# Layer 1's attention written out with two convolution passes, and two-byte tables in the routing

## The chip, the cores and the metric

The kernel runs on one core of a Trainium2 chip. The metric is device time in microseconds (us) of one execution. TensorE (PE, matrix products), VectorE (DVE), ScalarE (ACT), GpSimd (POOL) and SyncE (SP, which here only issues DMAs) run side by side and wait for each other through semaphores. Each engine works through its own instructions in order.

## The reference, cut to what matters

A batch of 16 samples with 102 tokens of 192 features goes through four layers, each an attention and a feed-forward part. The change touches the attention of layer 1 and the routing ahead of the experts in layers 0 and 1.

```python
# layer 1, attention (12 heads of 16 features); then h = h + out
qkv = layernorm(h, ln_g, ln_b) @ qkv_w.T + qkv_b             # q, k, v
attn = einsum('bhnd,bhmd->bhnm', q, k) * D ** (-0.5)
kernel = ones((3, 3)); kernel[1, 1] = 0                      # the eight neighbours
neigh = conv(attn, kernel, padding='SAME')
attn = softmax(attn - 0.2 * neigh)
out = einsum('bhnm,bhmd->bhnd', attn, v)

# layers 0 and 1, feed-forward: 8 experts, the best 2 of each token
top_logits, top_idx = top_k(xn @ gate_w, 2)
y = sum over the two of  gate * (act(xn @ w1[e]) @ w2[e])    # 1632 tokens x 2 = 3264 rows
```

The convolution needs no pass over the scores. The 3x3 sum of q.k is (sum of three neighbouring q).(sum of three neighbouring k), so each head takes 32 partitions instead of 16: the first 16 hold q and 1.2 k, the other 16 hold the sums of three q and -0.2 times the sums of three k.

## The kernel before, in words

`build` runs the layers one after the other, each in a block that all engines enter and leave together.

**Layer 1's attention**, `neighbour_attention` (L1020), works on pairs of samples, 8 pairs, "n" or "i" being the pair and "j" or "side" the sample in it. For each pair POOL gathers the experts' results of layer 0 back (`take_rows_back`, 4 indirect DMAs, L1294). DVE adds them into `h` (`add_rows_back`, L1329), takes mean and variance (`begin`), POOL raises the variance to -0.5 (`norm.pool`, L269), and DVE scales the rows into `z` (`end`, L264). PE transposes `z` (L1102), ACT copies the result to `xT` (L1220). PE multiplies it with the weights for q, k (`projected`, L1109, three blocks of 128 outputs for each) and v (`values`, L1122), and always splits the 192 inputs into two halves of 96. ACT copies q and k to `raw_q` and `raw_k` (L1226). DVE makes `qT` and `kT` from them in three passes (`mix`): raw times an own weight (L1353), plus the left neighbour (L1355), plus the right one (L1358).

For each sample PE then forms the scores (`scores`, L1137), DVE takes the maxima (L1364), PE turns them (L1145), ACT copies them (L1244), PE forms the scores again by key (L1153) and subtracts the maxima (L1158), ACT takes the exponentials (L1249), PE multiplies with v (`outputs`, L1167), ACT copies (L1254), PE turns back (`outputs_back`, L1176), DVE divides by the sums (L1371, L1373) and adds to `h` (`add_up`, L1379).

The order is written out by hand as a software pipeline. A prologue enters pairs 0 to 2, and then PE, ACT and DVE each run a loop of four rounds (`Fori(0, B // 4)`, L1198, L1265, L1402) over two pairs. Step i, j of the loop handles the output of sample 2i+j, the scores of the next sample, the projections of pair i+2 and the entry of pair i+3. The loop runs the same for all pairs, so in the last rounds it also handles pairs 8, 9 and 10, which hold zeros (`PADS`). PSUM is shared: the scores of the next sample overwrite the banks in which the q blocks (or k blocks) of pair i+2 stood, so `scores` waits for ACT's copies of them, and for DVE's copy of v (L1345).

**The routing**, in `routed_experts` (L2176), turns the two chosen experts of each token into a list of 33 tiles of 128 rows. DVE works out a slot for each token and choice. Then it writes two tables as 0 and 1 in bf16: `at_tile` (which of 33 tiles, L2587, multiplied with sample and token numbers into `named`, L2590 and L2592) and `at_row` (which of 128 rows, four instructions, L2595). PE multiplies them, 32 products (L2425), which gives the token of each slot; DVE makes `tokens` from it (L2610, L2612), POOL gathers the rows of the first tiles (L2344), and PE starts with the experts (L2356, L2368). After the tables DVE also works out which expert owns each tile (`owner`, L2599 to L2607); SP waits for it (`owner_ready`) to load the first three tiles' weights (L2288). PE waits for `tokens_ready` and then runs 12 dummy products (`fill`, L131), which write what nobody reads. Before that PE has 28 more at the start of the block, as `neighbour_attention` has 60.

Of the kernel before, what the change touches and what calls it, by code (L numbers as in the profile page):

```python
# [74 lines left out]
    "l1a": [("wq", K, C * HT * 128), ("wk", K, C * HT * 128), ("wv", K, C * D), ("bq", 128, HT), ("bk", 128, HT),  # L75
            ("bv", L, D), ("g", K, C), ("b", K, C), ("mix", 128, 4)],
# [29 lines left out]


class Steps:

    def __init__(self, eng, sem, before=0):
        self.eng, self.sem, self.before, self.n = eng, sem, before, 0

    def done(self, ins):
        ins.then_inc(self.sem, 1)
        self.n += 1

    def wait(self):
        self.eng.wait_ge(self.sem, self.before + self.n)  # L120
# [111 lines left out]


class Norm:


    def __init__(self, m, g, name, twice=False):
        times = 1 + twice
        self.twice = twice
        self.stats = m.sb(name + "_stats", [L, 2, 6])  # L240
        self.moments = m.sb(name + "_moments", [L, 2, 2])
        self.shifted = m.sb(name + "_shifted", [L, times, 2])
        self.rstd = m.sb(name + "_rstd", [L, times, 2])
        self.pause = m.sb(name + "_pause", [1, 1])
        self.neg_half = g["const"].at("neg_half16")[:, 0:2 * times].rearrange("p (a n) -> p a n", a=times)
        self.var_ready, self.rstd_ready = m.sem(name + "_var_ready"), m.sem(name + "_rstd_ready")

    def begin(self, dve, steps, src):

        for j in range(2):  # L250
            steps.done(dve.bn_stats(self.stats[:, j, :], src[j]))
        steps.wait()
        dve.memset(self.pause[:, :], 0.0)
        for j in range(2):
            steps.done(dve.bn_aggr(self.moments[:, j, :], self.stats[:, j, :]))
        steps.wait()
        last = dve.tensor_scalar(self.shifted[:, 0, :], self.moments[:, :, 1], EPS, None, ALU.add)
        if self.twice:
            last = dve.tensor_scalar(self.shifted[:, 1, :], self.moments[:, :, 1], 1.0 + EPS, EPS * EPS, ALU.mult, ALU.add)
        last.then_inc(self.var_ready, 1)  # L260
# [759 lines left out]
def neighbour_attention(nc, g, phase, experts):  # L1020
# [12 lines left out]
    with ExitStack() as stack:  # L1033
# [35 lines left out]
        def banked(j):  # L1069

            return ps[0:L, j, :, 0:HT * L].rearrange("p r (t n) -> p r t n", t=HT)
# [2509 lines left out]
```

## Time and profile before

| | us |
|---|---|
| median of 3 runs | 1826.01 |
| lowest and highest | 1823.01, 1833.23 |
| the profiled execution's own time | 1823.17 |
| its span | 1821.5 |
| layer 0's routing, within the span | 193.6 to 239.7 |
| layer 1's attention, within the span | 395.8 to 559.4 |
| layer 1's routing, within the span | 559.4 to 608.0 |

The profile is one execution recorded by the hardware. Its page has a table of busy time by engine and a strip of the span in 40 slices. The trace can be asked for groups of instructions by line, for who waited for whom, for the instructions in order of time, and for the busy time within given stretches, with the TensorE clock that was granted there (1.00 is 2.4 GHz, 0.50 is 1.2 GHz).

### The profile page before, as it was taken

To read this page: it belongs to the slowest core of one execution; us is meant where nothing else is said; L and a number is where in the kernel's file an instruction comes from. 1 tells how busy PE (TensorE), PEld (TensorE's weight loads), DVE (VectorE), ACT (ScalarE), POOL (GpSimd) and SP (SyncE) were. 2 spreads that over 40 slices of the span, in tenths; PEclk is the share of its full clock that TensorE was granted. 3 is DMA by queue.
4 is the path that set the end of the run, shared out by engine and by line. 5 is a ranking of instruction groups with operands and counts; after the bars stand their busy time and mean duration, and the time that the engine had idled before them with its cause. 6 is when DMAs were issued, how large, how long until landed. Compare 5 with 4: busy or idle time off the path is not lost. (4 is left out here: it accounts for less than half of the span.)

```text
span 1821.5 us, 35955 instructions
## 1 busy us (share of the span) xinstructions
PE 1619.2 (89%) x13405; PEld 1136.1 (62%) x13425; DVE 1020.2 (56%) x2819; ACT 749.2 (41%) x1439; POOL 557.3 (31%) x530
## 2 busy tenths in 40 slices
PE   7999689997996799979888877999999998889996
PEld 5677479976775699757645553222224775558886
DVE  2487722225888322258525665888886776942221
ACT  1266123323542111135524544899994553211111
POOL 1231022226001242265101112555553101325543
PEclk9999689997997899979889999999999998989998
DMA  6000445521004455212010114999992004026662
GB/s 227 1 2 2 159 159 182 183 88 44 1 0 163 158 182 182 91 29 76 35 46 1 42 51 138 385 395 370 360 327 103 2 2 151 4 72 187 187 186 35
DMA packets 97448, 228.04 MB, mean 125 GB/s; under 512 B 24298, under 2 KB 55754, under 8 KB 96394
## 3 DMA queue, kind: packets, MB, share of 16 engines
q1 hardware_dynamic: 77527, 206.13, 32.0%
q0 software_dynamic: 19552, 19.63, 4.4%
q8 instruction: 100, 1.64, 0.4%
q14 instruction: 59, 0.48, 0.1%
q10 hardware_dynamic: 210, 0.15, 0.0%
HBM read 198.91 MB, written 26.56 MB: 124 GB/s over the span
## 5 line engine op out<-in xcount | busy, mean ns | idle before, releaser
L2845 ACT ACTIVATE l2s_hidden<-ps,pack_l2f 128x816 f32<-128x816 f32 x256 | 226.8, 937 | 19.0 <-PE ps L2769 9.7
L2864 POOL TENSOR_TENSOR l2s_gated<-l2s_hidden,l2s_whole 128x408 f32<-128x408 f32 x128 | 136.7, 1068 | 104.0 <-PE ps L2777 104.0
L2887 DVE TENSOR_TENSOR l2s_gated<-l2s_hidden,l2s_whole 128x816 f32<-128x816 f32 x128 | 143.4, 1120 | 28.1 <-ACT l2s_hidden L2845 25.1
L2344 POOL DMA_INDIRECT l_xt<-rows_in,l_tokens x66 | 63.2, 957 | 250.8 <-PE ps L2357 193.6
L2385 PE MATMUL ps<-l_down,l_hidden 128*128 x792 | 139.8, 327 | 0.0
L2385 PEld LDWEIGHTS ps<-l_down,l_hidden 128*128 128x128 f32 x792 | 127.3, 190 | 0.4
L131 PE MATMUL ps<-pack_const 128*128 128x512 bf16 x366 | 98.2, 427 | 22.7 <-PEq L165 6.0
L2368 PE MATMUL ps<-l_xtT,l_up 128*128 128x128 f32 x792 | 101.2, 278 | 3.4 <-DVE l_xtT L2620 3.4
L2368 PEld LDWEIGHTS ps<-l_xtT,l_up 128*128 128x128 f32 x792 | 98.2, 194 | 4.5 <-DVE l_xtT L2620 4.5
L2464 ACT ACTIVATE l_hidden<-ps,l_down 128x128 f32<-128x128 f32 x198 | 54.6, 375 | 91.6 <-PE ps L2373 91.6
L3199 POOL DMA_INDIRECT out<-l3c_part,l3c_chosen_place x32 | 57.1, 1785 | 98.6 <-DVE l3c_part L3318 90.0
L3156 ACT ACTIVATE l3c_expert_gate<-ps 128x204 f32<-128x204 f32 x96 | 27.5, 338 | 145.1 <-PE ps L3092 145.1
L131 PEld LDWEIGHTS ps<-pack_const 128*128 128x128 bf16 x386 | 40.0, 107 | 75.5 <-issue 41.2
L2467 ACT ACTIVATE l_hidden<-ps 128x384 f32<-128x384 f32 x66 | 28.8, 488 | 139.7 <-PE ps L2373 139.7
L3328 DVE TENSOR_TENSOR l3c_expert_hidden<-l3c_expert_gate,ps 128x204 f32<-128x204 f32 x96 | 30.9, 364 | 98.1 <-ACT l3c_expert_gate L3156 98.1
L2880 DVE TENSOR_TENSOR l2s_gated<-l2s_hidden,ps 128x408 f32<-128x408 f32 x128 | 73.3, 572 | 15.5 <-ACT l2s_hidden L2845 9.9
L2620 DVE TENSOR_SCALAR l_xtT<-ps,pack_l0r 128x128 f32<-128x128 f32 x66 | 24.1, 406 | 78.6 <-PE ps L2357 78.6
L2620 DVE TENSOR_SCALAR l_xtT<-ps,pack_l1r 128x128 f32<-128x128 f32 x66 | 24.0, 406 | 77.8 <-PE ps L2357 77.8
L3105 PE MATMUL ps<-l3c_wd,l3c_expert_hidden 128*102 128x192 f32 x384 | 65.0, 326 | 0.0
L2791 PE MATMUL ps<-l2s_gated,early_down 128*32 128x408 f32 x512 | 58.5, 530 | 5.0 <-POOL l2s_gated L2864 3.5
L2373 PE MATMUL ps<-l_xtT,l_up 64*128 64x128 f32 x792 | 62.7, 291 | 0.0
L3105 PEld LDWEIGHTS ps<-l3c_wd,l3c_expert_hidden 128*102 128x102 f32 x384 | 61.4, 168 | 0.2 <-issue 0.2
(514 smaller groups left out, 3664.0 us busy)
## 6 DMA issues: line engine op xcount, KB each, us to landing
l2s_whole<-g_whole SPq DMA_DIRECT2D x128, 612.0 KB, 7.1
l_up<-in_l_up SPq DMA_DIRECT2D x66, 576.0 KB, 3.8
l3c_wg<-in_l_gate SPq DMA_DIRECT2D x16, 576.0 KB, 4.9
l3c_wu<-in_l_up SPq DMA_DIRECT2D x16, 576.0 KB, 6.5
l3c_wd<-in_l_down SPq DMA_DIRECT2D x16, 576.0 KB, 3.9
slots_out<-l_y SPq DMA_DIRECT2D x66, 96.0 KB, 2.3
l_down<-in_l_down SPq DMA_DIRECT2D x8, 675.0 KB, 7.9
l_down<-in_l_down SPq DMA_DIRECT2D x8, 576.0 KB, 8.0
```

Of the source, the lines that this page charges most:

```text
L131: pe.matmul(bank, halves[:, 0:128], halves[:, :], start=True, stop=True)
L2344: pool.indirect_dma_start(xt[:, i % 3, :], None, xs, bass.IndirectOffsetOnAxis(ap=tokens[:, i:i + 1], axis=0))\
L2368: pe.matmul(hid_bank(i, half)[:, t * 128:(t + 1) * 128], up[:, i % 3, n * 128:(n + 1) * 128], xtT[:, i % 2, 0, :], start=(t == 0), stop=Fa ...
L2373: last = pe.matmul(hid_bank(i, half)[:, t * 128:(t + 1) * 128], up[rows, i % 3, F + t * 128:F + (t + 1) * 128], xtT[rows, i % 2, 1, :], st ...
L2385: last = pe.matmul(y_bank(i), hidden[:, i % 2, t, :], wd[:, t * D:(t + 1) * D], start=(t == 0), stop=(t == FM - 1))
L2791: last = pe.matmul(sums[row:row + HP, :], down[2 * r + odd][:, pair, t, :], gated[:, (4 * n + 2 * pair + c) % ring, :], start=(odd == 0 an ...
L2845: act.activation(hidden[:, p % kept, :, :], ps[:, 0, 2 * (p % 2):2 * (p % 2) + 2, 0:NG], ACT.Gelu_apprx_tanh, bias=w.at("b1")[:, s * MT + ...
L2864: pool.tensor_tensor(gated[:, (4 * n + 1) % ring, :], hidden[:, 2 * n % kept, 1, :], whole[:, n % ahead, 0, :], ALU.mult).then_inc(late_re ...
L2880: dve.tensor_tensor(gated[:, 4 * n % ring, :], hidden[:, 2 * n % kept, 0, :], gate_bank(n), ALU.mult).then_inc(gated_ready, 1)
L2887: dve.tensor_tensor(gated[:, at:at + 2, :], hidden[:, (2 * n + 1) % kept, :, :], whole[:, n % ahead, 1:3, :], ALU.mult).then_inc(gated_rea ...
L3105: last = pe.matmul(part_bank(e)[:, a * D:(a + 1) * D], expert_hidden[:, e % 2, t, a, :], wd[:, e % RING, t, :], start=(t == 0), stop=(t == ...
L3199: pool.indirect_dma_start(table, bass.IndirectOffsetOnAxis(ap=chosen_place[:, a, e:e + 1], axis=0), part[:, e % 2, a, :], None, compute_op ...
```

## The change

**Layer 1's attention.** The loops become plain code for 16 samples (`for s in range(B)`), and the work on pairs 8 to 10 is gone. The 192 inputs are split into 128 and 64: a product over 128 rows, and one over 64 rows that is placed in the upper or lower half of the array, so that two of them (one with v, one with q or k; or two blocks) can stand beside each other. The 64-feature half of z is turned by products with the identity into both halves of the partitions. The k weight (1.2 and -0.2) goes into ACT's copy, `raw` gets a zero column at both ends, and the own-weight pass is gone: two passes remain. ACT takes the exponentials of sample 0 before it copies q and k of pair 1. POOL takes over `h += o` (`add_up`), DVE's division waits for it two samples later (`h_added`), and POOL issues the gathers of pair i+4 at step i instead of all at the start. The norm keeps three sets of moments (`PairNorm`, which the other attentions use already).

**The routing.** The tables are laid out with 8 tokens innermost, and all their operands become two bytes wide: `rows_8` and `sample_8` are made by POOL at the start of the block, `splitf` is bf16. PE reads the tables with a step of 8 elements. The owners are worked out before the ranks, and the fill has 10 products and stands before the wait for `tokens_ready`.

```diff
 # neighbour_attention, tensor engine
-                for c in range(C):
-                    for j in range(2):
-                        last = pe.transpose(zT_at(side)[:, ...], z[:, par, j, c * K:(c + 1) * K], ident[0:L, 0:L])
+                for j in range(2):
+                    pe.transpose(zT_at(side)[:, j * L:(j + 1) * L], z[:, n % 2, j, 0:WIDE], ident[0:L, 0:L])
+                for j in range(2):
+                    for a in range(2):
+                        last = pe.matmul(zT_at(side)[half_rows(a), (2 + j) * L:(3 + j) * L], z[:, n % 2, j, WIDE:D],
+                                         ident[0:L, 0:L], start=True, stop=True, tile_position=(0, REST * a))
+            def first_block(wt, side, j, bank=2):
+                pe.matmul(v_at(side, bank), xT[:, 0, j, :], wv[:, 0, :], start=True, stop=False)
+                wide_part(wt, side, 0)
+                pe.matmul(v_at(side, bank), xT[half_rows(0), 1, j, :], wv[half_rows(0), 1, :], start=False, stop=True,
+                          tile_position=(0, 0)).then_inc(v_ps, 1)
+                rest_part(wt, side, 0, 1)
+            def other_blocks(wt, side, done):
+                for t in (2, 1):
+                    wide_part(wt, side, t)
+                rest_part(wt, side, 2, 1)
+                rest_part(wt, side, 1, 0).then_inc(done, 1)
 # its order at the start
+            first_block(wq, 1, 0, bank=2)
+            scores_by_key(0)
+            other_blocks(wq, 1, q_ps)
             pe.wait_ge(q_ready, 2)
+            first_block(wk, 1, 1, bank=3)
+            other_blocks(wk, 1, k_ps)
-            with pe.Fori(0, B // 4) as two:
+            for s in range(B):
+                n, j = s // 2 + 2, s % 2
+                outputs(s)
+                if n < pairs and not j:
+                    transposes(n, 0)
+                if s + 1 < B:
+                    scores(s + 1)
+                outputs_back(s)
+                if n < pairs:
+                    pe.wait_ge(xT_ready, n + 1)
+                    first_block(wk if j else wq, j, j)
+                if s + 1 < B:
+                    top_turned(s + 1)
+                    scores_by_key(s + 1)
+                if n < pairs:
+                    other_blocks(wk if j else wq, j, k_ps if j else q_ps)
 # scalar engine: exponentials_by_key(0) now ahead of q_copies(1, 1) and k_copies(1)
 # GpSimd
+            def add_up(s):
+                pool.wait_ge(o_ready, s + 1)
+                pool.tensor_tensor(h[:, s, :], h[:, s, :], o[:, s % 2, :], ALU.add).then_inc(h_added, 1)
+            for i in range(pairs):
+                if i + 4 < pairs:
+                    take_rows_back(i + 4)
+                for j in range(2):
+                    add_up(2 * i + j)
+                if i + 3 < pairs:
+                    norm.power(pool, i + 3)
 # vector engine, mix
-                steps.done(dve.tensor_scalar(dst, raw, own_w, None, ALU.mult))
-                dve.scalar_tensor_tensor(dst[:, :, 1:L], raw[:, :, 0:L - 1], side_w, dst[:, :, 1:L], ALU.mult, ALU.add)
-                dve.scalar_tensor_tensor(dst[:, :, 0:L - 1], raw[:, :, 1:L], side_w, dst[:, :, 0:L - 1], ...)
+                dve.scalar_tensor_tensor(dst, raw[:, :, 0:L], beside, raw[:, :, 1:L + 1], ALU.mult, ALU.add)
+                dve.scalar_tensor_tensor(dst, raw[:, :, 2:L + 2], beside, dst, ALU.mult, ALU.add)
 # routed_experts
+            pool.tensor_copy(rows_8[:, :, :], iota.unsqueeze(2).broadcast_to([L, 128, 8])).then_inc(counted, 1)
+            pool.tensor_copy(sample_8[...], const.at("sample")).then_inc(counted, 1)
-                last = pe.matmul(ps[:, 1, 2, 0:2 * TILES], at_row[:, n, :], named[:, n, :, :], ...)
+                last = pe.matmul(ps[:, 1, 2, 0:2 * TILES], at_row[:, n // 8, :, n % 8], named[:, :, n // 8, :, n % 8], ...)
             last.then_inc(tokens_ps, 1)
+            fill(pe, g, ps[:, 0, 0, :], 10)
             pe.wait_ge(tokens_ready, 1)
-            fill(pe, g, ps[:, 0, 0, :], 12)
 # vector engine: the four owner instructions (L2599 to L2607) now ahead of the rank (L2569)
-            for n in range(0, 2 * B, 8):
-                dve.tensor_tensor(at_row[:, n:n + 8, :], iota.unsqueeze(1).broadcast_to([L, 8, 128]),
-                                  splitf[:, 1, n:n + 8].unsqueeze(2).broadcast_to([L, 8, 128]), ALU.is_equal)
+            for n in range(4):
+                dve.tensor_tensor(at_row[:, n, :, :], rows_8[:, :, :],
+                                  splitf[:, 1, n, :].unsqueeze(1).broadcast_to([L, 128, 8]), ALU.is_equal)
```

## Rows read from the trace of the kernel before

**Rows 1.** Waits, 447 to 559 us: waiter <- releaser: total us, times, longest.

```profile
PE ps L1137 <- ACT l1a_raw_q L1226: 3.4, 4, 0.9
```

**Rows 2.** Groups by line, VectorE, 447 to 559.2: count, busy, mean ns.

```profile
L1379 DVE TENSOR_TENSOR h<-h,l1a_o 102x192 f32 x16 | 5.6, 349 | 0.0
...
L1353 DVE TENSOR_SCALAR l1a_qT<-l1a_raw_q,pack_l1a 128x612 f32<-128x612 f32 x8 | 4.3, 533 | 0.0
```

**Rows 3.** Order of time, two samples of the loop: start, duration, engine, line.

```profile
464.53 0.80 PE L1137 MATMUL ps<-l1a_kT,l1a_qT 32*102 32x102 f32 x24 [0.79 <-DVE l1a_v L1345]
...
470.89 0.56 PE L1102 MATMUL ps<-pack_const,l1a_z 102*96 102x102 f32 x4
...
471.85 0.80 PE L1137 MATMUL ps<-l1a_kT,l1a_qT 32*102 32x102 f32 x24 [0.40 <-ACT l1a_raw_k L1226]
...
476.10 1.25 ACT L1249 ACTIVATE l1a_pT<-ps 102x612 f32<-102x612 f32 x2 [0.90 <-PE ps L1158]
...
477.72 1.07 ACT L1226 ACTIVATE l1a_raw_q<-ps,pack_l1a 128x204 f32<-128x204 f32 x3 [0.38 <-PE ps L1109]
...
479.12 0.80 PE L1137 MATMUL ps<-l1a_kT,l1a_qT 32*102 32x102 f32 x24 [0.85 <-ACT l1a_raw_q L1226]
```

**Rows 4.** Order of time, first output, first and second scores of the loop.

```profile
438.11 0.74 PE L1167 MATMUL ps<-l1a_pT,l1a_v 102*32 102x102 f32 x24 [2.48 <-ACT l1a_pT L1249]
...
440.64 1.38 PE L1137 MATMUL ps<-l1a_kT,l1a_qT 32*102 32x102 f32 x24
...
450.23 0.80 PE L1137 MATMUL ps<-l1a_kT,l1a_qT 32*102 32x102 f32 x24 [0.85 <-ACT l1a_raw_q L1226]
```

**Rows 5.** By stretch: us, busy of five engines, granted clock, DMA share, GB/s.

```profile
440.00:447.00 7.00, 7.00 (x74) 5.85 (x73) 4.80 (x9) 1.35 (x3) 5.48 (x6) 0.60 0.18 46
...
454.20:468.50 14.30, 13.45 (x212) 10.76 (x208) 12.35 (x34) 6.93 (x16) 1.04 (x1) 1.00 0.01 2
...
241.00:242.00 1.00, 1.00 (x7) 0.78 (x8) 0.00 (x0) 0.00 (x0) 0.00 (x0) 0.50 0.24 78
```

**Rows 6.** Order of time, last output, last division, next block's start.

```profile
549.60 0.73 PE L1167 MATMUL ps<-l1a_pT,l1a_v 102*32 102x102 f32 x24
...
559.48 0.11 DVE L2517 MEMSET l_before<- 102x64 f32 x1 [0.36 <-PEq L1033]
```

**Rows 7.** Order of time, layer 0's attention: split products, POOL's addition.

```profile
115.56 0.57 PE L597 MATMUL ps<-pack_const,l0f_z 102*64 102x102 f32 x8
...
120.63 1.59 PE L607 MATMUL ps<-l0f_xT,pack_l0f 128*128 128x204 f32 x8
...
109.49 0.96 PE L612 MATMUL ps<-l0f_xT,pack_l0f 64*128 64x204 f32 x8
...
110.79 0.86 POOL L861 TENSOR_TENSOR x<-x,pack_l0f 102x384 f32<-102x384 f32 x1
```

**Rows 8.** Order of time, layer 0's routing.

```profile
224.11 1.26 DVE L2590 TENSOR_TENSOR l_named<-x,pack_const 102x1056 bf16<-102x1056 bf16 x1
...
225.28 0.49 DVE L2592 TENSOR_SCALAR l_named<-x,pack_const 102x1056 bf16<-102x1056 bf16 x1
...
225.69 4.62 DVE L2595 TENSOR_TENSOR x<-pack_const,l_splitf 102x1024 bf16<-102x1024 f32 x4
...
231.67 0.20 DVE L2612 SCALAR_TENSOR_TENSOR l_tokens<-l_token_sums 128x33 uint32<-128x33 f32 x1
...
238.43 0.30 PE L2356 MATMUL ps<-pack_const,l_xt 128*128 128x128 f32 x1 [1.21 <-DMA l_xt<-rows_in,l_tokens]
```

**Rows 9.** Order of time, layer 1's routing: owners, tokens, first transposes.

```profile
600.21 0.41 DVE L2599 TENSOR_TENSOR l_passed<-pack_const,l_tiles_of 1x264 f32<-1x264 f32 x1
...
601.64 0.20 DVE L2612 SCALAR_TENSOR_TENSOR l_tokens<-l_token_sums 128x33 uint32<-128x33 f32 x1
...
606.72 0.30 PE L2356 MATMUL ps<-pack_const,l_xt 128*128 128x128 f32 x1
```

More of the change, by code:

```diff
@@ L231, in _ @@
                 dve.tensor_tensor(emb[:, q, :], ps[0:GB * NP, 0, q, 0:D], bias[:, :], ALU.add).then_inc(emb_ready, 1)
[L234 to L248, printed above, removed]
-        for j in range(2):
[L251 to L260, printed above, removed]
-    def apply(self, dve, i, src, dst, time=0):
-        dve.wait_ge(self.rstd_ready, i + 1)
-        return [dve.tensor_scalar(dst[j], src[j], self.moments[:, j, 0:1], self.rstd[:, time, j:j + 1],
-                                  ALU.subtract, ALU.mult) for j in range(2)]
-    def pool(self, pool, i):
-        pool.wait_ge(self.var_ready, i + 1)
-        pool.tensor_tensor(self.rstd[:, :, :], self.shifted[:, :, :], self.neg_half, ALU.pow).then_inc(self.rstd_ready, 1)
 def retention(nc, g, dram):
@@ L1284, in relay @@
                 sp.sem_inc(rows_back, 1)
-            for n in range(B // 2):
+            for n in range(pairs):
                 relay(n)
-            sp.sem_inc(rows_back, PADS // 2)
         @block.gpsimd
@@ L1317, in _ @@
-            dve.sem_inc(o_ready, freed)
-            enter_own = 10
-            def pair(n):
-                return [ds(2 * n + j, 1) for j in range(2)]
-            def add_rows_back(n, steps):
+            steps = Batch(dve, dve_steps)
+            dve.tensor_scalar(k_bias[:, :], w.at("bk"), w.at("mix")[:, 1:2], None, ALU.mult).then_inc(const_ready, 1)
+            for raw in (raw_q, raw_k):
+                last = dve.memset(raw[:, :, :, :], 0.0)
+            last.then_inc(const_ready, 1)
@@ L1347, in mix @@
[L1347 to L1351 removed]
+                dve.tensor_tensor(v[:, n % 2, j, :, 0:HD], heads, w.at("bv", H), ALU.add).then_inc(v_ready, 1)
@@ new lines, in entered @@
+            def entered(n):
+                add_rows_back(n)
+                begin(n)
+                end(n)
+            entered(0)
+            entered(1)
+            kept_values(0, 0, 0, 3)
+            kept_values(0, 1, 1)
+            mix(0, 0)
+            mix(0, 1)
+            maxima(0)
+            entered(2)
+            kept_values(1, 0, 1, 2)
+            mix(1, 0)
+            kept_values(1, 1, 1, 3)
+            for s in range(B):
+                i, j = s // 2, s % 2
+                if s + 1 < B:
+                    maxima(s + 1)
+                divide(s)
+                if j:
+                    if i + 3 < pairs:
+                        begin(i + 3)
+                    if i + 2 < pairs:
+                        kept_values(i + 2, 1, 1)
+                    if i + 3 < pairs:
+                        end(i + 3)
+                    if i + 2 < pairs:
+                        mix(i + 2, 0)
+                else:
+                    if i + 1 < pairs:
+                        mix(i + 1, 1)
+                    if i + 3 < pairs:
+                        add_rows_back(i + 3)
+                    if i + 2 < pairs:
+                        kept_values(i + 2, 0, 0)
```

457 lines of the change are left out of this document (194 added, 263 removed).

## Prediction, made before the changed kernel was run

> **What bounds the kernel now.** I read the trace in this order. First the order of time, to find the stages that the change touches: layer 1's attention, and in layers 0 and 1 the stretch from the choice of experts to the first tile. Together they are 258 of 1821.5 us, and the rest of the program stays as it is. Then the waits and the groups by line in the attention, the loop sample by sample, and its two ends.
>
> In the loop, VectorE and TensorE are both nearly full: 12.35 and 13.45 of 14.30 us, at clock 1.00 [rows 5]. But neither share is the bound. The reader is to look at what ends the wait of the scores (L1137), because each sample's scores start the next round of a ring: scores, maxima, turning, subtraction, exponentials, outputs, next scores. From 464.53 to 471.85 is 7.32 us and from 471.85 to 479.12 is 7.27 us [rows 3]. At 464.53 the scores waited for VectorE's copy of v, at 479.12 for ScalarE's copies of q, whose exponentials had ended at 477.35; the latter happens in every second pair [rows 1, 3]. So VectorE and ScalarE are late in turns, and an edit that relieves one of them leaves the other. From the second scores at 450.23 to the last outputs at 549.60 are 99.4 us [rows 4, 6], that is 13 samples at 7.21 and 5.7 us from scores to outputs.
>
> At the start, the first outputs (438.11) waited 2.48 us for exponentials, the scores of sample 1 then ran at the low clock (1.38 us against 0.80), and 9.6 us passed to the next ones [rows 4, 5]. At the end, 9.9 us pass between the last outputs and the next block, though the last division is over at 554.0 [rows 6]: the rest is work on pairs that don't exist.
>
> **The change, part by part.** All sums are against the profiled execution: 1823.17 us, with 1821.5 us of span.
>
> *The loop.* VectorE loses two own-weight passes of 0.53 us and two additions of 0.35 us for each pair, 1.8 us in all [rows 2]. That ends the waits for its copy of v. The additions go to GpSimd, where half of the 0.86 us that 384 columns took is 0.43 us [rows 7], beside four gathers for each pair; the division waits for them two samples later, some 14 us, so I cost this wait at nothing. If GpSimd came late by more than that, each microsecond would count fully. What is late next is ScalarE's copies of q. They waited 0.38 us for TensorE's last blocks [rows 3]. These blocks took 1.65 us; now they are two wide products, 1.59 / 4 = 0.40 us each, and two of 64 rows, 0.96 / 4 = 0.24 us each [rows 7], together 1.3 us, over before the exponentials end. So that step falls from 7.27 to 6.9 us. The other step contains the transposes: 0.56 us now [rows 3], and then half of that for the 128 wide part and 0.57 us for the rest [rows 7], 0.3 us more, starting at 470.89: scores at 471.75 instead of 471.85, 7.2 us. A pair costs 14.1 instead of 14.4 to 14.6; I take 13.95, since the loop's own turn also goes. The bounds are 14.5 (another wait takes over) and 13.3 (scores right behind outputs, with neither copies nor transposes late). Five pairs to sample 12 save 2.3 us. Samples 13 to 15 have no projections, copies or transposes ahead of their scores, and take about 6.35 us instead of 7.21: 2.6 us. Sum: **-4.9 us**, bounds -2 and -8.
>
> *Its start.* The two removed passes lie on the way to the first scores (-1.0 us). The exponentials of sample 0 now run beside the projections of pair 1, and the 2.48 us wait goes [rows 4]; against that stand the turning with more products and a longer wait for the copies of q. I get the scores of sample 1 about 3.3 us earlier. If the clock is then up, the 9.6 us to the next scores become 7.3: -2.3 us more [rows 4, 5]. Taken: **-5 us**, bounds -2 (clock still down) and -7.
>
> *Its end.* After the last outputs (0.73 us) come a copy, turning back, the division, and GpSimd's addition. Today the division ends 4.4 us after the outputs start, with the maxima of a seventeenth sample and copies of q in the way. I put it at 2.6 us, plus 0.5 for the addition and 0.35 for the change of block: 3.4 instead of 9.9 us [rows 6]. **-6.5 us**, bounds -4.6 (division as late as now) and -7.
>
> *The routing, twice.* The tables are two instructions of 1056 columns and four of 1024. The slope of such an instruction between 192 and 1056 columns is (1.26 - 0.35) / (1056 - 192) = 1.05 ns a column [rows 2, 8]. Half of that is 0.55 us for each of six: -3.3 us. No row shows a two-tensor instruction at two columns a beat. The bounds are nothing gained, and the one-tensor form's 0.49 us for 1056 columns [rows 8], -4.5 us; I take the half, since two tensors have to be read.
>
> The Trainium skill, VectorE: DVE Perf Modes, perf-mode tier table, has `tensor_tensor` at twice the rate when all operands are two bytes wide and at the single rate otherwise. The row that this can be held against has bf16 result and table but an f32 factor, and took 1.26 us [rows 8], which agrees with its second half. By the rule the six cost what I take.
>
> TensorE now reads both tables with a step of 16 bytes. Its products are eight for each `at_row` instruction and fit in its 1.16 us today; at 0.6 us they would be the bound if slowed. No row has such a read. I take no loss, and up to +2.4 us a layer as the bound (a doubled time for the products).
>
> The Trainium skill, SBUF: State Buffer, section on its two separate sides, says that SBUF has lines of 16 bytes, and that each access which crosses to a new line pays. Here each element would. By it the saving in the tables could vanish; this is the third rival.
>
> The owners, 1.2 us from 600.21 to the end of their four instructions [rows 9], move ahead of the tables. There they delay everything, while now they overlap PE's last products in part: +0.85 us. In return SP can load the first three tiles' weights some 9 us earlier, on idle DMA queues. POOL's `rows_8` copy comes before the first variance and is hidden. Behind the tokens, the first transposes came 6.8 us later in layer 0, waiting for the gather, and 5.1 us in layer 1, behind 12 dummy products [rows 8, 9]. With weights out of the way and the fill ahead of the wait, I take 4.6 us for both: -2.2 and -0.5 us. Sum for the two layers: -6.6 + 1.7 - 2.7 = **-7.6 us**, bounds +3 and -11.
>
> Together -4.9 - 5 - 6.5 - 7.6 = -24 us: 1799.2 us against the profiled 1823.17. The median before is 2.8 us above that execution, the lowest run 0.2 below. I put the changed kernel's median at **1801 us**, 1.4% below the median before.
>
> **The rivals.**
> 1. *The ring is shorter than I think*: with VectorE relieved, the scores follow right behind the outputs, 13.3 us a pair, and the clock stays up at the start. For it: VectorE stood in several rings at once. Against: ScalarE's copies of q come after the exponentials in any case [rows 3]. Another -5: 1796 us.
> 2. *The start stays cold and the loop keeps its 14.4 us*, because a copy or the longer transposes replace the wait for v. Then only the ends, the last samples and the routing gain: -2.6 - 2 - 6.5 - 7.6, 1804 to 1806 us.
> 3. *The tables gain nothing*: single rate, or TensorE's stepped reads as the new bound. The routing then gives about -1 instead of -7.6: 1808 us. With the clock falling in layer 1 too, 1810. In layer 0 it fell to 0.50 at 241 us, in the midst of the first tile, after TensorE had stood before and behind the first transposes [rows 5, 8]; now the fill ends earlier in both. I price it at what the cold start cost one sample, 2.3 us [rows 4].
> 4. *Slower*: the written-out attention runs at the low clock. TensorE is less dense than 13.45 of 14.30 us, since two 64-row products share the array. Cold, a sample took 9.6 instead of 7.3 us [rows 4, 5]; for 13 samples +30 us: 1831 us. It decides once about a third of the samples run cold, 24 / 2.3 = 10 of them for no gain at all. Against it: the fall at 440 us came after a wait of 2.48 us and another for the transposes, and the ring leaves TensorE no gap over about 1 us.
> 5. *The change doesn't do what it says*, as when the written-out code stalls on its instructions. Layer 0's attention is written out and shows no such waits. About 1823.
>
> **How the numbers follow.** Forecast 0.57 (1796 to 1806), rival 1 0.12, rival 2 0.12, rival 3 0.12, rival 4 0.04, rival 5 0.03. The range is 1790 to 1812: it takes in rivals 1 to 3 and most of the bounds. A change of 0.5%, 9 us, is about what a measurement of this kernel can tell from none. Forecast and rivals 1 to 3 all lie below 1817, so faster 0.92, same 0.04, slower 0.04.
>
> **What would show each step.** In the changed profile: L1167 to the next block's start about 3.4 us; scores to scores 6.9 and 7.2 us in the loop and 6.35 for the last three; the own-weight pass gone and the second scores near 445; clock 1.00 from there; the `at_row` comparisons at 0.6 us and the eight products behind them still at 0.6; the first transposes 4.6 us behind the tokens. I would be wrong if the wait of the scores moved to a place that I did not name, if the tables kept their 1.15 us, or if the clock in the attention fell below 1.00 after 450 us.

## The result, and the profile after

Eleven runs of the changed kernel have a median of 1813.1 us, ten of the kernel before 1827.4 us (an eleventh took 5250 us and is left out of the ratio). The ratio is 0.9936, 95% interval 0.9913 to 0.9960. A second series of twelve runs gave 1816.5 against 1826.7 us, 0.9930 (0.9904 to 0.9957). So the change makes the kernel faster by 0.65 to 0.7%, about 12 us. I had forecast 24 us and 1801 us, with a range up to 1812: the sign was right, the size half of what I had said, and the median lies just above the range.

The profiled execution of the changed kernel took 1823.34 us (span 1821.3), as long as the profiled one of before. To see why, I cut both spans where TensorE's first instruction of each block starts. "Touched" are the three blocks that the change touches, "others" is the rest of the span, whose code is the same.

| us | routing and experts, layer 0 | attention, layer 1 | routing and experts, layer 1 | touched | others |
|---|---|---|---|---|---|
| before | 202.1 | 163.6 | 201.6 | 567.3 | 1254.2 |
| after | 198.0 | 160.9 | 200.2 | 559.1 | 1262.2 |

The touched blocks gained 8.2 us and not 24. In this pair of executions the 8.2 us are taken up again by 8.0 us more in identical code. The largest piece of it stands in one place, the last 14 us ahead of the block at 1398 us. The windows (columns: stretch, its length, busy time and count of PE, PEld, DVE, ACT, POOL, PE's granted clock, DMA share, GB/s) of the kernel before and of the changed one:

```profile
1384.00:1398.00 14.00, 12.01 (x55) 7.13 (x58) 5.60 (x10) 2.27 (x4) 0.29 (x1) 1.00 0.00 0
```

```profile
1377.00:1398.00 21.00, 19.41 (x66) 10.58 (x59) 6.38 (x12) 2.27 (x4) 0.82 (x3) 0.67 0.00 0
```

The changed kernel reached these products 6.6 us earlier, then ran most of them at the low clock, and left them 0.8 us earlier.

**The attention's end.** TensorE's instructions in the order of time, from the scores of sample 13 on (start, duration, engine, line, operation, and in brackets how long the engine had stood and for whom). L1093 are the scores, L1127 the outputs:

```profile
522.69 0.80 PE L1093 MATMUL ps<-l1a_kT,l1a_qT 32*102 32x102 f32 x24 [1.08 <-ACT l1a_raw_k L1201]
525.10 0.48 PE L1101 MATMUL ps<-pack_const,l1a_top 102*128 102x102 f32 x3 [1.15 <-DVE l1a_top L1334]
528.25 1.25 PE L1127 MATMUL ps<-l1a_pT,l1a_v 102*32 102x102 f32 x24 [1.37 <-ACT l1a_pT L1212]
529.42 1.38 PE L1093 MATMUL ps<-l1a_kT,l1a_qT 32*102 32x102 f32 x24
538.08 1.37 PE L1093 MATMUL ps<-l1a_kT,l1a_qT 32*102 32x102 f32 x24
545.54 1.25 PE L1127 MATMUL ps<-l1a_pT,l1a_v 102*32 102x102 f32 x24 [1.37 <-ACT l1a_pT L1212]
```

The reader is to see three gaps of 1.08, 1.15 and 1.37 us within 7 us, where transposes and projections used to stand, and the next products at 1.25 us instead of 0.73: the clock is down. The window of the tail, before and after, has 1.00 and 0.51 (the last number but two):

```profile
527.00:552.00 25.00, 22.87 (x369) 18.32 (x368) 21.27 (x51) 12.93 (x31) 1.32 (x2) 1.00 0.00 0
```

```profile
527.00:552.00 25.00, 15.06 (x199) 10.13 (x199) 5.02 (x11) 5.82 (x11) 1.76 (x3) 0.51 0.00 1
```

The last scores come 8.66 us behind the ones before, not 6.35. The same step takes 8.64 to 8.66 us in each of the eight other profiles of this code without dummy products in the tail. Behind the last outputs follow GpSimd's addition and the next block:

```profile
548.96 0.59 POOL L1262 TENSOR_TENSOR h<-h,l1a_o 102x192 f32<-102x192 f32 x1 [6.75 <-DVE l1a_o L1345]
552.49 1.04 POOL L2286 CAST l_rows<-pack_const 102x1024 bf16<-102x1024 f32 x1 [2.94 <-POOLq L978]
552.52 8.95 PE L116 MATMUL ps<-pack_const 128*128 128x512 bf16 x28 [4.30 <-PEq L978]
```

The addition ends at 549.55, and nobody starts for 2.9 us. Before, VectorE's last instruction ended at 559.11 and the next block began at 559.48 [rows 6]:

```profile
558.26 0.85 DVE L1358 SCALAR_TENSOR_TENSOR l1a_qT<-l1a_raw_q,pack_l1a,l1a_qT 128x606 f32<-128x606 f32 x1
```

**Its start.** The clock fell while the first projections ran; four products took 1.73 us where they take 0.96 at 519 us. Below them the window of five microseconds behind:

```profile
407.17 0.57 PE L1065 MATMUL ps<-pack_l1a,l1a_xT 128*102 128x192 f32 x2 [1.39 <-ACT l1a_xT L1182]
409.04 1.73 PE L1055 MATMUL ps<-l1a_xT,pack_l1a 128*128 128x204 f32 x4
...
420.37 1.38 PE L1093 MATMUL ps<-l1a_kT,l1a_qT 32*102 32x102 f32 x24 [2.02 <-DVE l1a_kT L1329]
```

```profile
410.00:415.00 5.00, 5.00 (x17) 3.07 (x16) 2.21 (x11) 1.07 (x3) 3.48 (x4) 0.50 0.13 32
```

**Its loop.** The rows of one pair. From 479.49 to 486.59 are 7.10 us, to 494.05 7.46 us; the usual pair of steps is 7.10 and 7.37:

```profile
479.49 0.80 PE L1093 MATMUL ps<-l1a_kT,l1a_qT 32*102 32x102 f32 x24 [0.26 <-issue]
483.94 1.34 DVE L1300 SCALAR_TENSOR_TENSOR h<-rows_z,share,h 102x192 f32<-102x192 f32 x2
484.13 0.60 POOL L1262 TENSOR_TENSOR h<-h,l1a_o 102x192 f32<-102x192 f32 x1
485.99 0.35 DVE L1318 TENSOR_TENSOR l1a_v<-ps,pack_l1a 102x192 f32<-102x192 f32 x1
486.59 0.80 PE L1093 MATMUL ps<-l1a_kT,l1a_qT 32*102 32x102 f32 x24 [0.81 <-DVE l1a_v L1318]
494.05 0.80 PE L1093 MATMUL ps<-l1a_kT,l1a_qT 32*102 32x102 f32 x24 [0.35 <-DVE l1a_qT L1329]
```

**The tables**, in layer 1's routing (L2565 `at_tile`, L2573 the four `at_row`, L2393 TensorE's 32 products, L2580 the tokens, L2324 the first transposes):

```profile
587.09 0.71 DVE L2565 TENSOR_TENSOR x<-l_rows,l_splitf 102x1056 bf16<-102x1056 bf16 x1
588.86 2.50 DVE L2573 TENSOR_TENSOR x<-l_rows,l_splitf 102x1024 bf16<-102x1024 bf16 x4
589.69 4.17 PE L2393 MATMUL ps<-l_named,x 102*128 102x66 bf16 x32 [9.11 <-DVE x L2573]
593.90 0.23 DVE L2578 COPY l_token_sums<-ps 128x66 f32<-128x66 f32 x1 [2.54 <-PE ps L2393]
594.16 0.20 DVE L2580 SCALAR_TENSOR_TENSOR l_tokens<-l_token_sums 128x33 uint32<-128x33 f32 x1
598.10 0.45 PE L2324 MATMUL ps<-pack_const,l_xt 128*128 128x128 f32 x1
```

The four comparisons take 2.50 us instead of 4.62 [rows 8]. But 32 products in 4.17 us are 0.130 us each, where eight used to take 0.62, 0.077 each (granted clock 0.50 both times), and VectorE now waits 2.54 us for them.

### The profile page after: what moved, and what is told of

The parts are those of the page before. It is cut to its first block and busy times, and to the rows that moved or that the text cites. A ratio compares the mean times of both kernels' runs of the same rounds, so it can differ in the third digit from the quotient of the medians.

```text
span 1821.3 us, 35453 instructions
## 1 busy us (share of the span) xinstructions
PE 1635.0 (90%) x13338; PEld 1128.1 (62%) x13338; DVE 986.5 (54%) x2733; ACT 744.3 (41%) x1420; POOL 572.3 (31%) x547
## 5 line engine op out<-in xcount | busy, mean ns | idle before, releaser
L116 PE MATMUL ps<-pack_const 128*128 128x512 bf16 x382 | 107.4, 445 | 18.8 <-PEq L150 6.0
```

The costliest lines, as they stand in the source:

```text
L116: pe.matmul(bank, halves[:, 0:128], halves[:, :], start=True, stop=True)
```

## The experiments

All ratios are to runs of the kernel before on the same chip.

### Each half of the change alone

`e1` is the kernel before with layer 1's attention exchanged, `e2` the one with the routing exchanged in both layers.

> The kernel before with layer 1's attention alone changed (routing as before). In the changed kernel's profile this block took 160.9 us against 163.4, because the clock fell from 409 to 427 us and from 527 us on, and 2.9 us passed between GpSimd's last addition and the next block. Theory A (the clock's falls in the start and in the tail belong to this code): the block takes about 161 us again, with a fall in both places, and the kernel is 2 to 4 us faster than before. Rival B (they are a matter of where in time the block stands): one or both are gone or elsewhere, the block takes 153 to 157 us, and the kernel is 7 to 10 us faster. Both expect steps of the scores of 6.95 to 7.4 us and 2.9 us of block change.

Measured: 1821.6 us, ratio 0.9989 (0.9966 to 1.0012). The attention took 159.1 us. The last step of the scores was 8.65 us again and the block change 3.0 us:

```profile
548.90 0.59 POOL L1262 TENSOR_TENSOR h<-h,l1a_o 102x192 f32<-102x192 f32 x1 [6.75 <-DVE l1a_o L1345]
552.51 0.11 DVE L2480 MEMSET l_before<- 102x64 f32 x1 [3.68 <-PEq L978]
```

By their interval these runs alone can't tell the attention's gain from none; its block is 4.5 us shorter. The clock's fall in the tail belongs to the code (A). The one in the start does not stand still: the first scores came 24.7 us behind the block's start here, 28.7 us in the changed kernel, 25.2 before. And layer 1's routing, whose code is that of before, took 204.8 us here instead of 201.6: from the tokens to the first transposes 6.7 us passed instead of 5.1.

> The kernel before with the routing alone changed in both layers. Both theories expect 32 stepped products in 4.1 us that end the tables in place of VectorE, the tokens 0.6 us earlier in layer 0, the first transposes 3.1 us earlier in layer 0 and 1.7 us in layer 1. Theory A (the price of the change is local): 4 to 6 us faster than before, and the layer 1 block starts 4.4 us earlier. Rival B (a clock fall in the first tiles takes it back): under 2 us faster.

Measured: 1817.6 us, ratio 0.9967 (0.9943 to 0.9991). The products took 4.13 and 4.15 us. From the gate's result to the first transposes: 20.2 and 19.8 us, against 23.2 and 21.6 before. As A has it. So the routing carries about 6 us of the gain (2 to 10 by the interval), and the attention the 2 to 4.5 us that its runs and its block show.

### The block's end

```diff
                 for j in range(2):
-                    add_up(2 * i + j)
+                    if 2 * i + j + 1 < B:
+                        add_up(2 * i + j)
...
+            dve.wait_ge(o_ready, B)
+            dve.tensor_tensor(h[:, B - 1, :], h[:, B - 1, :], o[:, (B - 1) % 2, :], ALU.add)
```

> The changed kernel with the last of the 16 additions to h (sample 15) on VectorE instead of GpSimd. Theory A (a block whose last instruction is GpSimd's ends 2.5 us later than one whose last is VectorE's): from the end of the last addition to the next block 0.4 us instead of 2.9 us, the addition 0.35 instead of 0.59 us: 2.7 us faster than the changed kernel. Rival B (the 2.9 us are the time in which the queues fetch the code behind the long written-out block, or another engine's): the next block starts 0.2 us earlier or not at all.

```profile
548.30 0.36 DVE L1387 TENSOR_TENSOR h<-h,l1a_o 102x192 f32<-102x192 f32 x1
548.93 1.04 POOL L2289 CAST l_rows<-pack_const 102x1024 bf16<-102x1024 f32 x1 [7.33 <-POOLq L978]
```

From the end of the addition to the next block 0.27 us instead of 2.9; from the last outputs to TensorE's start 4.4 us instead of 7.0. A holds: the written-out block is as long as in the changed kernel, so 2.6 of the 2.9 us were the price of GpSimd being the last. The run as a whole, 1816.4 us, ratio 0.9959 (0.9940 to 0.9978), can't show 2.7 us; the rows can.

### The clock in the tail

```diff
                 outputs_back(s)
+                if n >= pairs and s + 1 < B:
+                    small_fill(s + 1, 16)
...
+                elif s + 1 < B:
+                    small_fill(s + 1, 22)
```

`small_fill` issues so many bf16 products of 128x104 into `ps[:, 1 - s % 2, 2, 408:512]`, columns that nothing uses.

> The changed kernel with dummy products in samples 12 to 14's gaps: 16 of 104 columns behind the turning back and 22 behind the scores by key, into 104 unused columns. Theory A (TensorE's gaps of 1.1 and 1.4 us in each of the last samples let the clock fall to 0.50 at 527 us): the clock stays at 1.00 to the end of the attention, the last steps of the scores are 6.4 to 6.7 us instead of 8.66, and the last outputs come 4 to 5 us earlier. Rival B (the fall has another ground, or the fill is itself in the way): clock 0.50 as before or steps over 7.4 us, no gain.

```profile
525.35 0.90 PE L1141 MATMUL ps<-pack_const 128*128 128x104 bf16 x16
526.65 0.48 PE L1101 MATMUL ps<-pack_const,l1a_top 102*128 102x102 f32 x3 [0.41 <-DVE l1a_top L1343]
528.36 1.18 PE L1141 MATMUL ps<-pack_const 128*128 128x104 bf16 x22
529.80 0.73 PE L1127 MATMUL ps<-l1a_pT,l1a_v 102*32 102x102 f32 x24 [0.26 <-ACT l1a_pT L1221]
530.46 0.80 PE L1093 MATMUL ps<-l1a_kT,l1a_qT 32*102 32x102 f32 x24
536.69 0.80 PE L1093 MATMUL ps<-l1a_kT,l1a_qT 32*102 32x102 f32 x24
```

The last two steps are 6.22 and 6.23 us, the clock stays at 1.00, and the attention takes 154.4 us. 1808.0 us, ratio 0.9910 (0.9877 to 0.9942). A holds: with the gaps filled there is no fall. From the scores of sample 12 to the last outputs 25.4 us pass instead of 30.2, so it had cost 4.8 us.

### TensorE's stepped reads

`e5` puts 2 tokens innermost in the tables and `e10` 4, so TensorE steps by 4 and by 8 bytes; the changed kernel steps by 16, the one before by 2.

```diff
-        named = m.sb("named", [L, 2, 4, TILES, 8], BF16)
-        rows_8 = m.sb("rows_8", [L, 128, 8], BF16)
+        named = m.sb("named", [L, 2, 16, TILES, 2], BF16)
+        rows_2 = m.sb("rows_2", [L, 128, 2], BF16)
...
-                                 named[:, :, n // 8, :, n % 8], start=(n == 0), stop=(n == 2 * B - 1))
+                                 named[:, :, n // 2, :, n % 2], start=(n == 0), stop=(n == 2 * B - 1))
```

> The changed kernel with 2 tokens innermost in the tables instead of 8, so TensorE reads them with a step of 4 bytes instead of 16. Theory A (the price of TensorE's stepped reads grows with the lines of 16 bytes touched): a product takes under 0.09 us instead of 0.129, eight of them 0.6 to 0.7 us, VectorE's tables stay at 0.6 us an instruction, and the tokens come 1.5 us earlier in each layer; 3 us faster than the changed kernel. Rival B (any step other than one costs the same): 0.129 us a product, no gain. Rival C (VectorE loses its double rate with pairs innermost): 1.15 us for each instruction of 1024 columns, 2 us slower in each layer.

```profile
225.68 2.49 DVE L2573 TENSOR_TENSOR x<-l_rows,l_splitf 102x1024 bf16<-102x1024 bf16 x4
226.51 2.34 PE L2393 MATMUL ps<-l_named,x 102*128 102x66 bf16 x32 [9.12 <-DVE x L2573]
228.89 0.23 DVE L2578 COPY l_token_sums<-ps 128x66 f32<-128x66 f32 x1 [0.72 <-PE ps L2393]
```

VectorE keeps its 0.62 us an instruction, TensorE follows in 2.34 us, and from the tables to the tokens 5.24 us pass instead of 7.04, in both layers. The touched blocks take 553.8 instead of 559.1 us. 1813.7 us, ratio 0.9931 (0.9904 to 0.9959). A, as far as a step of 4 bytes goes.

> The changed kernel with 4 tokens innermost in the tables, a step of 8 bytes for TensorE. If the price grows with the lines of 16 bytes that a product touches (all at a step of 16, a quarter at a step of 4, which cost nothing), half of the elements touch a new line here: between 0.077 and 0.129 us a product, about 0.09 to 0.10. If it is a threshold in the step, 0.129 us, or nothing extra.

```profile
226.92 2.40 PE L2393 MATMUL ps<-l_named,x 102*128 102x66 bf16 x32 [9.11 <-DVE x L2573]
```

2.40 us (and 1814.1 us in its one run), hidden behind VectorE's 2.49: a step of 8 bytes costs nothing that this can show, one of 16 costs 0.05 us a product. My proportional estimate (0.09 to 0.10 us) was wrong; the price sets in between 8 and 16 bytes. The Trainium skill, SBUF — State Buffer, Door 1: The DMA port swizzle, has that a line of 16 bytes must be hit at least twice to be read at full rate. By that rule two hits at a step of 8 are free and one hit at 16 is not, and the runs agree. The note's example of a free step, 8 bf16 elements, doesn't hold here: that is the step of 16 bytes, and it cost 0.05 us a product.

### The additions on VectorE

`e6` puts all sixteen `h += o` on VectorE, behind its copy of v, as before the change, and drops the wait for `h_added`.

```diff
-                for j in range(2):
-                    add_up(2 * i + j)
...
                         kept_values(i + 2, 0, 0)
+                    add_up(s)
```

> The changed kernel with all 16 additions of the attention's result to h on VectorE, behind its copy of v, as in the kernel before. Theory A (GpSimd's addition runs at the same time as VectorE's and stretches both, 0.75 to 1.34 us for a pair of VectorE's row additions, which is what holds the v copy back and makes the step 7.10 instead of 6.95 us): the stretched instructions go back to 0.75 us, the steps are 6.95 and 7.37 us, 14.3 a pair instead of 14.45, and the block ends 2.5 us earlier behind the last addition; about 3 us faster. Rival B (VectorE has no room for 0.7 us more in a pair): steps of 7.3 us and more, the gain of the block's end eaten up.

```profile
481.83 0.74 DVE L1294 SCALAR_TENSOR_TENSOR h<-rows_z,share,h 102x192 f32<-102x192 f32 x2
483.28 0.35 DVE L1312 TENSOR_TENSOR l1a_v<-ps,pack_l1a 102x192 f32<-102x192 f32 x1
484.32 0.80 PE L1093 MATMUL ps<-l1a_kT,l1a_qT 32*102 32x102 f32 x24 [0.66 <-ACT l1a_raw_q L1191]
```

A holds. The steps are 6.95 and 7.37 us, the scores wait for ScalarE's copies of q and no longer for VectorE's copy of v, and the attention takes 157.2 us. In the changed kernel VectorE's row additions took 0.41 us as a rule and up to 1.01 us; here never over 0.48. The 0.60 us more is all of GpSimd's 0.595. In five other samples the addition met the passes of `mix` instead: there it took 1.12 to 1.40 us itself, and a pass 1.06 instead of 0.85. The Trainium skill, SBUF — State Buffer, section on its two separate sides, says that VectorE's instructions with two inputs in SBUF and GpSimd's share one pair of ports, which one of them holds for its whole instruction while the other stands; the rows agree. 1812.7 us, ratio 0.9941 (0.9911 to 0.9972).

### The owners and the fill

`e9` moves the four instructions of the owners back behind `at_row`. `e11` moves the fill:

```diff
-            fill(pe, g, ps[:, 0, 0, :], 10)
             pe.wait_ge(tokens_ready, 1)
+            fill(pe, g, ps[:, 0, 0, :], 12)
```

> The changed kernel with the owners back behind the at_row comparisons, where VectorE waits 2.5 us for TensorE's stepped products anyway, so their 1.3 us are hidden there. Theory A (the loads of the tiles' weights, which SP issues once the owners are known, are what held the first gather back in the kernel before, 6.7 us from tokens to the first transposes instead of 4.3): the tokens come 1.3 us earlier, but the first transposes 6 to 6.7 us behind them; 1 us slower in each layer. Rival B (the 6.7 us came from the 12 dummy products that stood behind the wait for the tokens, 5.1 us at the low clock): the first transposes stay 4.3 us behind the tokens; 1.3 us faster in each layer.

```profile
229.46 0.20 DVE L2581 SCALAR_TENSOR_TENSOR l_tokens<-l_token_sums 128x33 uint32<-128x33 f32 x1
236.90 0.45 PE L2324 MATMUL ps<-pack_const,l_xt 128*128 128x128 f32 x1 [3.48 <-DMA l_xt<-rows_in,l_tokens]
```

Tokens to first transposes: 7.4 and 7.8 us instead of 4.3 and 3.9, and TensorE waits for the gather. In all they came 2.0 and 2.6 us later, twice what A had, and the first tile's products ran cold (12 of them in 2.93 us; 2.32 in the changed kernel, 1.60 where all of it is warm). The rows of the weights' loads and of the gather:

```profile
228.91 2.63 SPq L2254 DMA_DIRECT2D l_up<-in_l_up  x3
230.56 1.23 POOL L2312 DMA_INDIRECT l_xt<-rows_in,l_tokens  x1 [25.89 <-DVE l_tokens L2581]
```

From 230 to 236 us the DMA engines are 0.91 busy, and TensorE gets the rows of the gather, issued 1.65 us behind the loads, only at 236.9. In the changed kernel the loads are issued at 223.14 and the gather at 232.14, with a DMA share of 0.00 from 230 to 233. So the weights' loads, issued late, hold the gather back, and the 1.2 us that the owners cost ahead of the tables buy over 3 us behind them. 1825.5 us, ratio 1.0009 (0.9981 to 1.0036); the two routing blocks take 404.7 us, 6.4 more. The runs show more loss (9 to 14 us, by what one sets them against) than the blocks; I have no reason for the rest.

> The changed kernel with the 12 dummy products behind the wait for the tokens, as in the kernel before. Theory A (the fill was no bound): the first transposes stay 4.3 us behind the tokens, or come when the 12 products end, 1.3 + 5.1 = 6.4 us behind them if they run at the low clock. I expect the second, 6.4 to 6.7 us, 2.2 us slower in each layer; that would show that the fill and not the loads held the first tile back. Rival B (the loads): 4.3 us.

Measured: 5.3 and 5.1 us, neither 6.4 nor 4.3. The fill took 4.90 and 4.55 us for the 11 products recorded, and the transposes followed it by its end. In layer 1 the 5.1 us are those of the kernel before, where they followed the fill's end too and waited for no gather. But the two blocks took 198.0 and 200.3 us, as in the changed kernel: the first tile then ran at the full clock. 1820.5 us, ratio 0.9954 (0.9926 to 0.9982). The place of the fill moves the first transposes by 1.0 to 1.2 us and is worth nothing in the block's time that these runs show.

### Together

`e7` has the edits of `e3`, `e4` and `e5`. `e8` has dummy products in the gaps of the attention's start as well, and `e12` the owners late on top.

```diff
             transposes(0, 0)
+            start_fill(22)
...
             transposes(1, 1)
+            start_fill(26)
             pe.wait_ge(const_ready, 3)
             scores(0)
+            start_fill(20)
             top_turned(0)
...
             other_blocks(wq, 1, q_ps)
+            start_fill(14)
             pe.wait_ge(q_ready, 2)
```

> The changed kernel with three edits together: last addition on VectorE, dummy products in the last samples' gaps, tables with 2 tokens innermost. Theory A (the three losses are separate): layer 1's attention takes 152 us from block to block if its start stays warm, 155 if not, the tokens come 1.5 us earlier in each layer; 9 to 11 us faster than the changed kernel, near 1803 us. Rival B (what is won is given back by falls of the clock further on, in code that none of the edits touches): under 5 us.

Measured: 1804.8 us, ratio 0.9887 (0.9855 to 0.9920); attention 151.2 us, touched blocks 544.0 us, 15.1 less than in the changed kernel, where `e3`, `e4` and `e5` won 3.1, 6.7 and 5.3 us. The three losses are separate.

> As the one with the three edits, and with dummy products of 104 columns in the gaps of the attention's start too: 22 while the first copies run, 26 before the scores of sample 0, 20 behind them, 14 before the keys of pair 1. Theory A (TensorE's gaps of 1.4 to 2 us there let the clock fall): clock 1.00 from 395 to 440 us, and the second scores 40 to 41 us behind the block's start instead of 43 to 44.6; 3 to 4 us faster than without. Rival B (the clock falls there anyway, after the gaps of ScalarE's and VectorE's chain, and the fill then takes twice its time and stands in the way): second scores as late or later, up to 3 us slower.

```profile
402.30 1.18 PE L1146 MATMUL ps<-pack_const 128*128 128x104 bf16 x22
403.75 0.57 PE L1065 MATMUL ps<-pack_l1a,l1a_xT 128*102 128x192 f32 x2 [0.27 <-ACT l1a_xT L1200]
413.04 0.80 PE L1093 MATMUL ps<-l1a_kT,l1a_qT 32*102 32x102 f32 x24 [1.32 <-DVE l1a_kT L1348]
426.30 0.80 PE L1093 MATMUL ps<-l1a_kT,l1a_qT 32*102 32x102 f32 x24 [0.16 <-issue]
```

```profile
410.00:415.00 5.00, 3.53 (x78) 3.03 (x76) 3.81 (x6) 1.69 (x5) 4.09 (x4) 1.00 0.23 55
```

The clock is 1.00 throughout, the second scores come 38.7 us behind the block's start, and the attention takes 146.3 us. In the profiled changed kernel the second scores came at 44.6 us; in the ten other profiles with the same start code at 40.3 to 43.8 us, so the dummy products in the start are worth 2 to 6 us. 1803.6 us, ratio 0.9870 (0.9827 to 0.9913), the lowest median of all and 20 us below the runs of before beside it (1823.4). The runs can't tell it from `e7` (1804.8); the touched blocks can, 539.2 against 544.0 us.

> All edits together: tables with 2 tokens innermost, last addition on VectorE, dummy products in the attention's start and end, and the owners behind the tables. Beside the kernel without the last of these (1803.6 us): if the loads are no bound, 0.6 us faster in each layer, 1802 us; if they are, 1.8 us slower in each, 1807 us. Layer 1's attention takes 146.3 us from block to block again.

Measured: 1807.8 us, ratio 0.9909 (0.9872 to 0.9945); attention 146.5 us, its second scores at 38.6 us, tokens to first transposes 6.6 us in layer 0 and 5.2 in layer 1, where 4.2 and 4.0 stood in `e8`. The two routing blocks take 9.8 us more than in `e8`, of which I had expected 3.6. The loads are a bound here too, and the owners belong ahead of the tables.

### The same kernels again

> The changed kernel once more, unedited. In its profile the blocks that the change touches were 8.2 us shorter than before, and all other blocks, whose code is the same, together 8.0 us longer, at a lower granted clock. Theory A (the falls of the clock in the other blocks differ from execution to execution and have nothing to do with the change): the touched blocks take 555 to 560 us again, the others anything from 1245 to 1262 us, near 1256 us. Rival B (the change moves the other blocks to where the clock falls more often): 1260 us or more again.

> The kernel before once more, unedited, for a second profile. Theory A (executions differ by falls of the clock): the other blocks differ from their 1254.2 us by several us, the touched ones from 567.3 by 3 us at most, all of it in the attention's start and the experts' first tiles. Rival B: 1254 us again, so that 8 us more in the changed kernel's profile are the change's.

| us | touched | others |
|---|---|---|
| before, second profile | 567.3 | 1258.9 |
| after, second profile | 559.6 | 1254.9 |

A holds both times. Over all fourteen experiments' profiles the others took 1244.6 to 1265.7 us with the same code, while the touched blocks of one kernel repeat to 0.5 us. That is closer than they always do: the attention as changed took 158.2 to 161.8 us in seven profiles, most of it in its start, and layer 1's routing as before 201.6 to 204.8 us in three. In the eleven runs of the changed kernel the time goes with the mean granted clock: 1806.1 us at 0.936, 1823.3 us at 0.918. So the 8.0 us belong to the execution that was profiled. What decides where the clock falls in those blocks stays open, and so does the difference between the 8 us of the touched blocks and the 12 us of the runs, whose two intervals begin at 7 and 8 us.

## Why the prediction came out wrong

From the rows of the two first profiles, against the steps of the prediction. Starts of blocks are TensorE's, so the end reads 10.1 us here and 9.9 in the prediction, which took VectorE's:

| term | forecast | measured |
|---|---|---|
| loop, second scores after the start to last outputs | -4.9 | +3.0 (99.4 to 102.4) |
| start, block to those scores | -5 | -2.6 (54.2 to 51.5) |
| end, last outputs to next block | -6.5 | -3.1 (10.1 to 7.0) |
| routing, from the choice of experts to the first transposes, both layers | -7.6 | -4.8 (-3.1, -1.7) |
| the rest of the routing blocks (ahead of the choice +0.7, tiles of the experts -1.3) | 0 | -0.6 |

**The loop.** The step that failed is "samples 13 to 15 take about 6.35 us instead of 7.21": from the scores of sample 12 to the last outputs I had 24.8 us, and 30.2 were measured, with the clock down from 527 us on. It is the largest single miss, 5.5 us. The ring itself was right: with the clock held up it is 6.22 us, and the stretch 25.4 (`e4`). I had counted the projections that vanish as time won and not as TensorE's work lost. My rival 4 named the low clock, and I put against it that the ring leaves no gap over about 1 us; the rows show 1.08, 1.15 and 1.37 us just where transposes and projections are gone. It struck the last two to three samples and not all 13. The other samples came 7.10 and 7.37 us apart instead of 6.9 and 7.2, ten samples in 72.2 us as before (72.0). "That ends the waits for its copy of v" failed: the scores at 486.59 still waited 0.81 us for it. 0.15 us of each pair is the collision of GpSimd's addition with VectorE (`e6`, where that wait is gone), for which my sum had no term; 0.26 us is TensorE's gap ahead of the scores behind the transposes, which was missing from my sum. With it the transposes gave back what the copies had won.

**The start.** Scores of sample 1 to those of sample 2 take 6.9 us, as said (7.3). But the first scores came 28.7 us behind the block's start instead of 25.2, not 1.0 earlier, and the scores of sample 1 at 44.6 as before: the first projections ran cold. This term depends on the execution: over the eleven profiles of this start code it comes to -2.6 to -6.9 us, and the profiled one was the slowest. So the start's miss of 2.4 us is in part bad luck of that profile, and the value taken lies in the midst of what the code does.

**The end.** The division was in time: from the start of the outputs 3.35 us, 0.9 of them the low clock in two groups of products, against the 2.6 forecast. What failed is "0.35 for the change of block", read from a block that VectorE ends [rows 6] and applied to one that GpSimd ends. It measured 2.9 us, and 0.27 with VectorE last (`e3`).

**The routing.** The double rate came as forecast: 0.71 and 0.62 us where 1.26 and 1.16 stood. "I take no loss" for TensorE's stepped reads was wrong: +1.8 us a layer (7.04 against `e5`'s 5.24 from tables to tokens), within the bound of 2.4 that I had given. This was rival 3's second mechanism at half its price: the tables still gained 1.4 us of the forecast 3.3, and 3.2 in `e5`. The owners cost what I took: 1.2 us ahead of the tables, less 0.4 behind them. The gain behind the tokens was right: 4.3 and 3.9 us instead of 6.8 and 5.1, forecast 4.6. Its cause in layer 0 is mostly the weights out of the gather's way (`e9`); 1.0 of the 2.5 us comes back with the fill behind the wait. In layer 1 it is the fill's place, as the prediction had it: with it behind the wait the 5.1 us are back (`e11`).

**The sum.** With the losses of its tail, start and end undone the attention takes 146.3 us (`e8`); 163.6 less my 16.4 is 147.2. That the two agree is luck: counted as in the table, `e8` has -8.6 in the start (forecast -5, bound -7), -1.9 in the loop (forecast -4.9, bound -2) and -6.9 in the end (forecast -6.5). The start won more than I had, with dummy products that the change doesn't have, and the loop less, because its pairs never got shorter. The forecast took the good value for the start, the tail, the block's end and TensorE's stepped reads at once, and each had its own way to fail. (24 us below the median of 1826 is 1802; I had written 1801.) The range left those falls to two rivals at 0.12 and 0.04, though the trace of before showed a fall in this block's start [rows 5].

## What to carry to other kernels

Here the work taken from TensorE's queue was also the work that had kept its clock up, and the fall cost 4.8 us in three samples: look at each stretch from which a change removes products, measure the gaps that are left, and put small dummy products there into unused PSUM columns. Let the last instruction of a block be another engine's than GpSimd's (2.6 us here). Issue large loads well before a gather that the next stage waits for, and not just ahead of it (3 us here). And where one engine writes a table for another, choose the innermost extent for both: two, four and eight two-byte elements all kept VectorE's double rate, but only two and four TensorE's speed.

## What the runs showed of the hardware

- A bf16 product with 128 columns of weights and 66 moving ones, both read at a step of 16 bytes, took 0.129 us; at steps of 2, 4 and 8 bytes it took 0.077 us or less. The granted clock was 0.50 in all of them.
- Behind a last instruction on GpSimd the next block began 2.9 to 3.0 us later, behind one on VectorE 0.3 to 0.4 us (`e3`, before).
- A two-input instruction of VectorE (102x192, 0.41 us) that met GpSimd's addition (0.595 us) took 1.01 us; where the addition started into VectorE's pass of 612 columns, it took 1.12 us and more itself.
- A gather of 128 rows issued 1.7 us behind three loads of weights, 576 KB each, held TensorE's next stage back until 7.4 us after the tokens began; with the loads over before it was issued, 4.3 us.
- The same code of some 1256 us took between 1245 and 1266 us from one execution to the next, with the mean granted clock between 0.918 and 0.943 over the whole program. One profiled execution can hide a change of 8 us or invent one. The durations of the touched blocks were steadier, but one attention code still took 158.2 to 161.8 us.
